# Attention blocks with (head, query) rows beside an LSTM recurrence, and an earlier output-gate product

## Chip, cores and metric

One core of a Trainium2 chip. The metric is the device time of one execution in microseconds, the median of three runs.

## The reference

Four sequences (B = 4) of S = 256 tokens with D = 128 features go through five stages; the last three are what the change is about.

1. An adaptive-layernorm transformer block in hyperbolic coordinates (16 heads), conditioned by one vector per sequence.
2. Causal attention with 16 heads of 8 features:

```python
Q, K, V = (x @ W_dq) @ W_uq, (x @ W_dkv) @ W_uk, (x @ W_dkv) @ W_uv      # each (B, S, 16, 8)
scores = einsum('bqhd,bkhd->bhqk', Q, K) / sqrt(8)
out = einsum('bhqk,bkhd->bqhd', softmax(where(causal, scores, -inf)), V).reshape(B, S, 128) @ W_o
```

3. The sum x + out, input of an LSTM of 128 units over the 256 tokens: `a = x_t @ Wx + b + h @ Wh`, then sigmoid and tanh gates. Step t needs h of step t - 1, and x_t needs the attention's output of token t.
4. A feed-forward block (128 to 512 to 128, GELU) on the LSTM's outputs, and a residual sum.

All tensors are float32.

## The kernel before, in words

Each engine has its own instruction list; semaphores join them. `big` is one large SBUF buffer, `bank` all eight PSUM banks. TensorE executes a float32 product as two passes, which the profile lists as two weight loads and two matmuls; a "pass" below is one of them.

**The front** (up to about 187 us) is the first stage, tiles of 128 tokens: two times `front`, attention or feed-forward, `join` on VectorE and ScalarE, with TensorE between. While VectorE is in the second `front`, ScalarE prepares the attention's and the LSTM's weights (L656 to L677). At the end of the front, TensorE turns the output weights W_o (L1308), waits for ScalarE's copy of them (L692), multiplies them with Wx (`wox`, L1310), waits for `tanh_out`, and fills the gates of the first 32 steps: biases, x @ Wx, h0 @ Wh (L1343 to L1347). Then it turns the first stage's result (L1351, waits for the first half of `join`'s output, `cond_out` 1) and begins the attention.

**The recurrence** is the loop over t of 256 steps in each of four engines' lists. In a step TensorE adds h @ Wh to the gates (12 passes, L1562 to L1564), ScalarE takes three tanh (L774 to L778), VectorE the cell state (L1136), ScalarE its tanh (L781), VectorE the new h (L1144) and the history (L1146). After these instructions each engine's list has its **jobs** of step t (`pe_jobs`, `act_jobs`, `vec_jobs`), which run while the others are in the chain of the step.

**The attention** is one of these jobs. Queries go in blocks of 32 tokens, called chunk c = 0 to 7; chunk c must be ready, with the gates made from it, before step 32 c. A block has c + 1 key blocks of 32. Rows of a score tile are (sequence, query), 4 x 32 = 128. A unit is some heads of a block: 4 heads for c below 4, 2 heads from there on. Units start every three steps from step 3 (`unit_at`); 44 of them run beside the recurrence, the last one starts in step 132. A unit m has

- step 0: `m_scores`, mask product (L1431), then for each head and sequence a product 32 columns wide in its own quarter of the array (L1436, `tile_position`); weights are the queries in `qz`, zero outside the head's 8 feature rows, moving data the keys of the sequence;
- step 1: VectorE takes the row maxima (`m_max`, L1070); steps 2 and 3: ScalarE the exponentials (L720);
- step 5: `m_turn`, four transposes of 128 columns on TensorE (L1449), step 6: VectorE copies them from PSUM (`m_weights`, L1079, 512 columns);
- step 7: `m_values`, for each head and sequence a product of 9 columns, 8 features and the sum of the weights (L1468), 16 products in all; steps 8 and 10, in a block's last unit: `m_norm`, `m_turn_out`, `m_oT`.

As units begin every third step, scores and the copy fall on steps with t = 0 mod 3, maximum and values on 1 mod 3, transposes on 2 mod 3. Other TensorE jobs: ten projections of the second half of the tokens (`PROJ`, every third step from step 2); and for the next chunk's gates, in steps 10 to 15 and 26 to 30 of each chunk, three bias products (L1315 to L1319), four products with x (L1322) and four with the attention's output (L1325). From step 146 on the feed-forward block takes the attention's place. The first block (L1356 to L1408, units 0 and 1) stands before the loop, in a form of its own with (sequence, query) rows, values held as block-diagonal `vd`.

**Queues.** SP issues, in order, for each block c from 1 on 16 transfers from `qT` into the ring `qz` (L499), one per head, block c after the scores of block c - 2. They follow the q half's ScalarE copy (L709). GpSimd's list ends with the low part of Wh (L549).

## Time and profile before

| | us |
|---|---|
| median of 3 runs (626.53 to 628.70) | 627.6 |
| profiled execution, its own time | 629.12 |
| its span, first to last instruction | 627.2 |
| mean granted TensorE clock | 0.622 of 2.4 GHz |
| busy: PE / DVE / ACT | 475.4 / 367.3 / 302.9 |

How to read it: PE is TensorE's matmuls, PEld its weight loads, DVE VectorE, ACT ScalarE, POOL GpSimd, SPq the queue of SyncE. The clock in slices is in tenths of full speed; it has two levels, 2.4 GHz (9 or 10 tenths) and 1.2 GHz (5 tenths). Matmuls overlap in the pipeline, so busy times of PE are not sums of useful work. A group `x4` in a timeline is four neighbours merged.

### The profile page before, as it was taken

The page shows a single profiled execution, that of the slowest core. Times are in us where ns is not written, and L with a number is a line of the kernel's source. Part 1 is how long each engine was busy: PE and PEld are TensorE (multiplying, and loading weights), DVE is VectorE, ACT ScalarE, POOL GpSimd, SP SyncE. Part 2 cuts the span into 40 slices and gives each one's busy share as a digit, 9 for nine tenths or more (in the row PEclk, how much of TensorE's full clock was granted, in tenths as well). Part 3 has the DMA queues.
Part 4 walks back from the last instruction along what each step waited for, and adds up shares of the span by engine and source line. Part 5 has one row for each costly group of instructions (what it writes and reads, how often), then busy time and mean ns, then how long its engine had stood idle before and what let it go on. Part 6 is the DMA issues. An engine that isn't in the chain of part 4 may idle for free.

```text
span 627.2 us, 17942 instructions
## 1 busy us (share of the span) xinstructions
PE 475.4 (76%) x6687; PEld 324.1 (52%) x6687; DVE 367.3 (59%) x2035; ACT 302.9 (48%) x1356; POOL 15.8 (3%) x36
## 2 busy tenths in 40 slices
PE   5973999107647898899999999898677768757746
PEld 2233334104535677666767666565455556545534
DVE  5367333894674556766676666666645555555553
ACT  4165785432324555645454444444454444444443
POOL 5000100030000000000000000000000000000000
PEclk9995999656957558855655555665555555555555
DMA  7200200000000000000000000000000000000000
GB/s 190 68 0 9 60 1 1 1 0 1 1 1 4 9 8 5 6 7 3 5 5 3 6 3 2 3 3 2 3 2 5 6 6 1 7 6 3 4 6 5
DMA packets 10884, 7.20 MB, mean 11 GB/s; under 512 B 2629, under 2 KB 9773, under 8 KB 10798
## 3 DMA queue, kind: packets, MB, share of 16 engines
q1 hardware_dynamic: 9742, 5.54, 3.5%
q8 instruction: 53, 0.87, 0.6%
q10 hardware_dynamic: 1056, 0.52, 0.3%
q14 instruction: 33, 0.27, 0.1%
HBM read 4.02 MB, written 0.52 MB: 7 GB/s over the span
## 4 chain that ended last, share of the span: by engine, by line
PE 54%; DVE 24%; ACT 15%; issue 5%; ACTq 0%; DVEq 0%
PE bank L1436 10%; PE bank L1562 7%; ACT hid_a L781 5%; DVE cell L1136 5%; PE bank L1449 5%; DVE hid L1144 4%; ACT keep L774 4%; PE bank L1322 3%; PE bank L1218 3%; PE bank L1564 3%; DVE cell_a L1128 2%; PE bank L1325 2%; PE bank L1206 2%; PE bank L1563 2%; PE bank L1162 2%
## 5 line engine op out<-in xcount | busy, mean ns | idle before, releaser
L1562 PE MATMUL bank<-hid,wha 128*128 128x4 f16 x1020 | 109.5, 173 | 70.1 <-DVE hid L1144 66.0
L1562 PEld LDWEIGHTS bank<-hid,wha 128*128 128x128 f16 x1020 | 89.1, 104 | 126.8 <-DVE hid L1144 120.3
L774 ACT ACTIVATE keep<-bank 128x4 f32<-128x4 f32 x256 | 44.4, 173 | 141.7 <-PE bank L1564 138.8
L1128 DVE SCALAR_TENSOR_TENSOR cell_a<-keep,cell 128x4 f32<-128x4 f32 x256 | 42.8, 167 | 110.9 <-ACT keep L774 109.6
L1563 PE MATMUL bank<-hid,whb 128*128 128x4 f16 x1020 | 103.6, 167 | 0.0
L1564 PE MATMUL bank<-hid,whn 128*128 128x4 f16 x1020 | 103.5, 166 | 0.0
L1563 PEld LDWEIGHTS bank<-hid,whb 128*128 128x128 f16 x1020 | 91.3, 107 | 2.2 <-issue 0.6
L781 ACT ACTIVATE hid_a<-cell 128x8 f32<-128x8 f32 x256 | 54.3, 212 | 73.8 <-DVE cell L1136 73.8
L1564 PEld LDWEIGHTS bank<-hid,whn 128*128 128x128 f16 x1020 | 87.3, 103 | 0.0
L1144 DVE TENSOR_TENSOR_SCAN hid<-hid_f,hid_a 128x20 f16<-128x20 f32 x256 | 51.2, 200 | 52.6 <-ACT hid_a L781 52.4
L1436 PE MATMUL bank<-kT,big 128*32 128x64 f32 (+6 forms) x896 | 66.4, 454 | 0.0
L1136 DVE TENSOR_TENSOR_SCAN cell<-cell_f,cell_a 128x16 f32<-128x16 f32 x256 | 49.1, 192 | 6.2 <-ACT cell_f L778 1.8
L778 ACT ACTIVATE cell_f<-bank 128x8 f32<-128x8 f32 x256 | 47.0, 184 | 0.3 <-PE bank L1325 0.3
L1449 PE MATMUL bank<-ident,p_mla 128*128 128x128 f32 (+3 forms) x176 | 44.5, 403 | 1.7 <-DVE qT L1090 1.7
L776 ACT ACTIVATE emit<-bank 128x4 f32<-128x4 f32 x256 | 44.3, 173 | 0.0
L1131 DVE TENSOR_SCALAR hid_f<-emit 128x8 f32<-128x8 f32 x256 | 43.7, 171 | 0.0
L1140 DVE RECIPROCAL hid_f<-hid_f 128x4 f32<-128x4 f32 x256 | 40.5, 158 | 0.4 <-issue 0.4
L720 ACT ACTIVATE p_mla<-bank,mx 128x64 f32<-128x64 f32 (+6 forms) x112 | 39.9, 378 | 0.0
L1436 PEld LDWEIGHTS bank<-kT,big 128*32 128x32 f32 x896 | 30.8, 156 | 12.9 <-issue 6.4
L1146 DVE TENSOR_TENSOR v_tm<-hid_f,hid_a 128x4 f32<-128x4 f32 x256 | 35.8, 140 | 0.1
L1468 PE MATMUL bank<-vaug,q_sq 128*32 128x9 f32 (+3 forms) x1408 | 31.3, 202 | 0.7 <-DVE q_sq L1079 0.5
L1079 DVE COPY q_sq<-bank 128x512 f32<-128x512 f32 (+3 forms) x46 | 30.9, 671 | 0.8 <-PE bank L1383 0.8
(271 smaller groups left out, 775.9 us busy)
## 6 DMA issues: line engine op xcount, KB each, us to landing
big<-qT SPq DMA_DIRECT2D x112, 4.0 KB
big<-big SPq DMA_DIRECT2D x16, 64.0 KB, 2.0
x_tm<-in_x ACTq DMA_DIRECT2D x2, 256.0 KB, 3.7
wf<-in_L_cond_w_f SPq DMA_DIRECT2D x2, 256.0 KB, 5.2
x_tb<-in_x SPq DMA_DIRECT2D x4, 128.0 KB, 2.8
out_y<-tb SPq DMA_DIRECT2D x7, 64.0 KB, 1.9
ada_w<-in_L_cond_w_ada SPq DMA_DIRECT2D x1, 384.0 KB
bf_all<-in_L_cond_b_f SPq DMA_DIRECT2D x1, 256.0 KB, 5.3
```

Source lines behind the costliest of these rows:

```text
L774: nc.scalar.activation(keep[:, k, :], keep_bank(c)[:, i], ACT.Tanh, scale=1.0 / A_SCALE).then_inc(keep_act, 1)
L776: nc.scalar.activation(emit[:, k, :], emit_bank(c)[:, i], ACT.Tanh, scale=1.0 / A_SCALE).then_inc(emit_act, 1)
L778: nc.scalar.activation(cell_f[:, k, :, 1:3].rearrange("p b s -> p s b"), new_bank(c)[:, i], ACT.Tanh, scale=1.0 / A_SCALE).then_inc(new_ac ...
L781: nc.scalar.activation(hid_a[:, k, :, 0:4:3], cell[:, k, :, 3].unsqueeze(2).to_broadcast([P, B, 2]), ACT.Tanh, scale=-1.0).then_inc(th_act, 1)
L1128: V.scalar_tensor_tensor(cell_a[:, k, :, 2], keep[:, k, :], 1.0, cell[:, 1 - k, :, 3], ALU.add, ALU.mult).then_inc(kept, 1)
L1136: V.tensor_tensor_scan(cell[:, k].rearrange("p b s -> p (b s)"), cell_f[:, k].rearrange("p b s -> p (b s)"), cell_a[:, k].rearrange("p b s ...
L1144: V.tensor_tensor_scan(hid[:, k].rearrange("p b s -> p (b s)"), hid_f[:, k].rearrange("p b s -> p (b s)"), hid_a[:, k].rearrange("p b s -> ...
L1436: ins = T.matmul(bank[q, m % 2, j * keys:(j + 1) * keys], qz[:, c % 2, heads[j], q], kT_tokens[:, b, 0:keys], start=False, stop=True, tile ...
L1449: ins = T.transpose(bank[0:rows, 2, i * P:(i + 1) * P], p_mla[:, m % 2, j * keys + kc * P:j * keys + kc * P + rows], ident[:])
L1562: T.matmul(acc, wha[:, gate, :], hid[:, k, :, 2], start=False, stop=True, skip_group_check=True)
L1563: T.matmul(acc, whb[:, gate, :], hid[:, k, :, 2], start=False, stop=True, skip_group_check=True)
L1564: ins = T.matmul(acc, whn[:, gate, :], hid[:, k, :, 4], start=False, stop=True, skip_group_check=True)
```

## The change

Score tiles of blocks 1 to 7 get rows (head r of a group, query), 4 x 32. A unit is now a group g of four heads (heads g, 4 + g, 8 + g, 12 + g) and all four sequences (blocks 1 to 3) or two of them (blocks 4 to 7). One product of full width, 128 columns, makes the scores of a sequence; half of them are issued in step 0, half in step 1. The exponentials are turned by VectorE in blocks of 32x32 from `p_mla` to `pt_mla` (step 5), which needs no TensorE transposes, no PSUM and no copy. The turned weights have keys of all four heads in the partitions, so the values are block-diagonal: `vd` holds for each sequence, key block and head its 32 x 9 values in that head's partitions and columns and zeros elsewhere; a value product has 36 columns, one for each key block and sequence, 32 wide, in step 8. `m_norm` moves to step 9, `m_turn_out` to 11, `m_oT` to 12.

`vd` is filled by SP: 12 transfers behind block 1's queries and 16 behind block 4's, 128 rows of 144 bytes each; the query transfers now move 32 pieces of 128 bytes instead of 8 of 512. GpSimd clears `vd` (8 memsets of 128x576 words, released by the first feed-forward product, and awaited by VectorE before the first block's values). The v projection of the first half moves from steps 2 and 5 to two places before the loop (`v_half`); the other projections move six steps up.

W_o is turned, copied and multiplied with Wx between the weight preparation's steps, during the second `front`; the first gates wait for `sq_in` (the scaled f2 output read out of its banks) instead of `tanh_out` and the late `wox`.

The diff, cut to its core:

```diff
-        UNITS = [(0, range(8 * i, 8 * i + 8)) for i in range(2)]
-        UNITS += [(c, range(h, h + n)) for c in range(1, CHUNKS) for n in [GROUP if c < GROUP else 2] for h in range(0, H, n)]
+        UNITS = [(0, 2 * i, None) for i in range(2)]
+        UNITS += [(c, g, range(b, b + n)) for c in range(1, CHUNKS) for n in [B if c < GROUP else B // 2] for g in range(NG) for b in range(0, B, n)]
-        PROJ = [("v", 0, 0), ("v", 0, 1), ("turn", 1, 0), ("turn", 1, 1), ("q", 1, 0), ("q", 1, 1), ("k", 1, 0), ("k", 1, 1),
+        PROJ = [("turn", 1, 0), ("turn", 1, 1), ("q", 1, 0), ("q", 1, 1), ("k", 1, 0), ("k", 1, 1),
@@ SP
-                    sp.dma_start(qz[rows, c % 2, h, :], flat(qT[rows])[:, c * P:(c + 1) * P]).then_inc(qz_fill[c % 2][h // GROUP], 16)
+                    r, g = divmod(h, GROUP)
+                    sp.dma_start(qz[rows, c % 2, :, g, QB * r:QB * r + QB], q_tokens[rows, c]).then_inc(qz_fill[c % 2][g], 16)
+                if c in (1, GROUP):
+                    f = c // GROUP
+                    if f == 0:
+                        sp.wait_ge(v_half_ready, 2)
+                        sp.wait_ge(vd_zero, 1)
+                        sp.wait_ge(ones_ready, 1)
+                    else:
+                        sp.wait_ge(proj_ready, len(PROJ))
+                    for kb in range(max(1, GROUP * f), GROUP * (f + 1)):
+                        for r in range(GROUP):
+                            keys = slice(QB * (kb % GROUP), QB * (kb % GROUP) + QB)
+                            sp.dma_start(vd[QB * r:QB * r + QB, :, kb, r].rearrange("p b g v -> p b (g v)"),
+                                         vm[keys, B * f:B * (f + 1), GROUP * r:GROUP * (r + 1), :].rearrange("p b h v -> p b (h v)")).then_inc(vd_fill[f], 16)
@@ GpSimd
+            pool.wait_ge(f1_mm, 1)
+            for b in range(B):
+                for c in range(0, CHUNKS, 4):
+                    ins = nc.gpsimd.memset(vd[:, b, c:c + 4], 0.0)
+            ins.then_inc(vd_zero, 1)
@@ ScalarE
             nc.scalar.activation(wdT[:], bank[0:64, 4, 0:P], ACT.Copy).then_inc(wdT_ready, 1)
+            act.wait_ge(wo_turned, 1)
+            nc.scalar.activation(woT, bank[:, 7, 0:P], ACT.Copy).then_inc(woT_ready, 1)
...
             nc.scalar.mul(h0[:], condT[:], H_SCALE).then_inc(w_ready, 1)
+            act.wait_ge(wox_mm, 1)
+            nc.scalar.activation(wox[:].rearrange("p g n -> p (g n)"), bank[:, 7, :], ACT.Copy).then_inc(wox_ready, 1)
...
-            act.wait_ge(wo_turned, 1)
-            nc.scalar.activation(woT, bank[:, 4, 0:P], ACT.Copy).then_inc(woT_ready, 1)
-            act.wait_ge(wox_mm, 1)
-            nc.scalar.activation(wox[:].rearrange("p g n -> p (g n)"), bank[:, 5, :], ACT.Copy).then_inc(wox_ready, 1)
...
+                if t in (0, 1):
+                    yield lambda: v_half(t)
@@ VectorE
-            go(V.tensor_copy(vd[:, :, :, HD], ...), vd_ready)
+            vec.wait_ge(vd_zero, 1)
+            for b in range(B):
+                go(V.tensor_copy(vd[:, b, 0, :, :, HD], ...), vd_ready)
...
             def m_weights(m):
-                V.tensor_copy(pt_mla[0:rows, m % 2, 0:cols], bank[0:rows, 2, ...][:, 0:cols]).then_inc(mt_ready, 1)
+                n = len(UNITS[m][2]) * keys_of(m)
+                vec.wait_ge(mp_ready, m + 1)
+                vec.wait_ge(mpv_mm, m - 1)
+                V.transpose(pt_mla[:, m % 2, 0:n], p_mla[:, m % 2, 0:n]).then_inc(mt_ready, 1)
@@ TensorE
             ins.then_inc(w_mla_mm, 1)
+            T.transpose(bank[:, 7, 0:P], wo_m[:], ident[:]).then_inc(wo_turned, 1)
             pe.wait_ge(ld_xtb, 64)
             turn8(lambda t: x_tb[:, t, :], 0, x_turned)
+            pe.wait_ge(woT_ready, 1)
+            pe.wait_ge(w_ready, 2)
+            T.matmul(bank[:, 7, :], woT, wx[:].rearrange("p g n -> p (g n)"), start=True, stop=True).then_inc(wox_mm, 1)
...
-            pe.wait_ge(tanh_out, 2)
-            pe.wait_ge(wox_ready, 1)
+            pe.wait_ge(sq_in, SQUARES_TO_F2)
...
+            def v_half(k):
+                for t in (2 * k, 2 * k + 1):
+                    ins = T.matmul(bank[:, 1, t * P:(t + 1) * P], vT[:, t, :], w_mla[:, 2, :], start=True, stop=True)
+                ins.then_inc(v_half_mm, 1)
             for m in range(FIRST_UNITS):
                 first_values(m)
+            v_half(0)
             m_turn_out(0)
+            v_half(1)
...
                 for j in range(n // 2 * part, n // 2 * (part + 1)):
-                    for b in range(B):
-                        q = slice(QB * b, QB * b + QB)
-                        ins = T.matmul(bank[q, m % 2, j * keys:(j + 1) * keys], qz[:, c % 2, heads[j], q], kT_tokens[:, b, 0:keys],
-                                       start=False, stop=True, tile_position=(0, QB * b), skip_group_check=True)
+                    ins = T.matmul(bank[:, m % 2, j * keys:(j + 1) * keys], qz[:, c % 2, bs[j], g, :], kT_tokens[:, bs[j], 0:keys],
+                                   start=False, stop=True, skip_group_check=True)
...
+                if m == FIRST_UNITS or (c == GROUP and g == 0):
+                    pe.wait_ge(vd_fill[c // GROUP], 16 * GROUP * (GROUP - 1 + c // GROUP))
+                for kb in range(c + 1):
+                    for j, b in enumerate(bs):
+                        at = (j * (c + 1) + kb) * QB
+                        n = GROUP * (HD + 1)
+                        ins = T.matmul(bank[QB * b:QB * b + QB, 4, n * g:n * (g + 1)], pt_mla[:, m % 2, at:at + QB], vd[:, b, kb, :, g, :],
+                                       start=(kb == 0), stop=(kb == c), tile_position=(0, QB * b))
...
+                for part, lag in ((0, 0), (1, 1)):
+                    m = unit_at(t, lag)
+                    if m is not None:
+                        yield lambda: m_scores(m, part)
+                n = unit_at(t, 8)
```

## Rows read from the trace of the kernel before

**Rows 1.** The page: busy time by engine, clock in 40 slices.
```profile
PE 475.4 (76%) x6687; PEld 324.1 (52%) x6687; DVE 367.3 (59%) x2035; ACT 302.9 (48%) x1356; POOL 15.8 (3%) x36
...
PEclk9995999656957558855655555665555555555555
```

**Rows 2.** Timeline, VectorE, L1144: start us, us, engine, line, operation, out<-in.
```profile
200.80 0.20 DVE L1144 TENSOR_TENSOR_SCAN hid<-hid_f,hid_a 128x20 f16<-128x20 f32 x1 [0.20 <-ACT hid_a L781]
...
476.49 0.20 DVE L1144 TENSOR_TENSOR_SCAN hid<-hid_f,hid_a 128x20 f16<-128x20 f32 x1 [0.20 <-ACT hid_a L781]
...
477.97 0.20 DVE L1144 TENSOR_TENSOR_SCAN hid<-hid_f,hid_a 128x20 f16<-128x20 f32 x1 [0.20 <-ACT hid_a L781]
...
620.03 0.20 DVE L1144 TENSOR_TENSOR_SCAN hid<-hid_f,hid_a 128x20 f16<-128x20 f32 x1 [0.20 <-ACT hid_a L781]
```

**Rows 3.** Timeline, TensorE, one attention unit of the last block.
```profile
431.25 1.09 PE L1449 MATMUL bank<-ident,p_mla 128*128 128x128 f32 x4
...
432.75 0.21 PE L1431 MATMUL bank<-mask,identb 128*128 128x64 bf16 x1
...
432.89 1.94 PE L1436 MATMUL bank<-kT,big 128*32 128x256 f32 x16
...
435.17 0.62 PE L1468 MATMUL bank<-vaug,q_sq 128*32 128x9 f32 x32
```

**Rows 4.** Timeline, VectorE, the same steps.
```profile
430.65 0.20 DVE L1144 TENSOR_TENSOR_SCAN hid<-hid_f,hid_a 128x20 f16<-128x20 f32 x1 [0.20 <-ACT hid_a L781]
...
430.82 0.69 DVE L1070 TENSOR_REDUCE mx<-bank 128x2 f32<-128x512 f32 x1
...
432.15 0.20 DVE L1144 TENSOR_TENSOR_SCAN hid<-hid_f,hid_a 128x20 f16<-128x20 f32 x1 [0.20 <-ACT hid_a L781]
...
433.63 0.20 DVE L1144 TENSOR_TENSOR_SCAN hid<-hid_f,hid_a 128x20 f16<-128x20 f32 x1 [0.20 <-ACT hid_a L781]
...
433.81 0.68 DVE L1079 COPY q_sq<-bank 128x512 f32<-128x512 f32 x1
...
435.98 0.20 DVE L1144 TENSOR_TENSOR_SCAN hid<-hid_f,hid_a 128x20 f16<-128x20 f32 x1 [0.20 <-ACT hid_a L781]
```

**Rows 5.** Timeline, TensorE, before the recurrence.
```profile
180.26 2.07 PE L1310 MATMUL bank<-wx,q_tm 128*128 128x512 f32 x2 [12.60 <-ACT q_tm L692]
...
183.36 0.80 PE L1322 MATMUL bank<-big,wx 128*128 128x128 f32 x2
...
187.41 1.09 PE L1351 MATMUL bank<-ident,v_tm 128*128 128x128 f32 x4
...
190.63 1.91 PE L1361 MATMUL bank<-w_mla,o_tm 128*128 128x128 f32 x8
```

**Rows 6.** Timeline, TensorE, the first block's values, and one pass of them.
```profile
196.57 0.34 PE L1393 MATMUL bank<-big,q_sq 128*32 128x36 f32 x16
...
L1393 PE MATMUL bank<-big,q_sq x32: 197/200/221, 196.6 to 197.3; 128*32 128x36 f32 x32
```

**Rows 7.** The page: the two scans; out<-in xcount | busy us, mean ns | idle before.
```profile
L1144 DVE TENSOR_TENSOR_SCAN hid<-hid_f,hid_a 128x20 f16<-128x20 f32 x256 | 51.2, 200 | 52.6 <-ACT hid_a L781 52.4
...
L1136 DVE TENSOR_TENSOR_SCAN cell<-cell_f,cell_a 128x16 f32<-128x16 f32 x256 | 49.1, 192 | 6.2 <-ACT cell_f L778 1.8
```

**Rows 8.** Timeline, VectorE, the last join, its first half of results.
```profile
182.69 1.14 DVE L943 SCALAR_TENSOR_TENSOR v_tm<-ta,small,tb 128x128 f32<-128x128 f32 x4
```

**Rows 9.** Windows: stretch, length, busy us of PE, PEld, DVE, ACT, POOL; PEclk, DMA share, GB/s.
```profile
183.80:193.40 9.60, 8.91 (x53) 7.72 (x52) 4.07 (x13) 3.42 (x11) 0.00 (x0) 0.50 0.00 0
193.40:200.20 6.80, 5.33 (x74) 3.06 (x66) 3.63 (x11) 2.23 (x7) 0.00 (x0) 1.00 0.02 5
```

**Rows 10.** SP's issues at L499 (ns min/median/max); landing of L484's transfers (us min/median/max).
```profile
L499 SPq DMA_DIRECT2D big<-qT x112: 624/624/1069, 196.3 to 356.1; - x112
...
DMA to landing us min/median/max: 2.0/2.0/2.2
```

**Rows 11.** Groups by line and shape: the weight loads of the eight products of rows 5.
```profile
L1361 PEld LDWEIGHTS bank<-w_mla,o_tm 128*128 128x128 f32 x8 | 1.8, 333 | 0.0
```

More of the change, by code:

```diff
@@ L224, in adaln_attention_lstm_ffn @@
         qz_zero = sem("qz_zero")
+        vd_zero = sem("vd_zero")
+        v_half_mm = sem("v_half_mm")
+        v_half_ready = sem("v_half_ready")
+        vd_fill = [sem("vd_fill_low"), sem("vd_fill_high")]
         ones_ready = sem("ones_ready")
@@ L365, in closes @@
         def closes(m):
-            return UNITS[m][1][-1] == H - 1
-        units_until = [sum(c <= k for c, _ in UNITS) for k in range(CHUNKS)]
+            return m == len(UNITS) - 1 or UNITS[m + 1][0] > UNITS[m][0]
+        units_until = [sum(c <= k for c, _, _ in UNITS) for k in range(CHUNKS)]
         ADA_PARTS = ((0, 2 * D), (2 * D, 6 * D))
@@ L418, in keys_of @@
             return QB * (UNITS[m][0] + 1)
-        def turns(m):
-            keys = keys_of(m)
-            return [(j, kc, min(P, keys - kc * P)) for j in range(len(UNITS[m][1])) for kc in range(1 + (keys > P))]
-        PROJ = [("v", 0, 0), ("v", 0, 1), ("turn", 1, 0), ("turn", 1, 1), ("q", 1, 0), ("q", 1, 1), ("k", 1, 0), ("k", 1, 1),
+        PROJ = [("turn", 1, 0), ("turn", 1, 1), ("q", 1, 0), ("q", 1, 1), ("k", 1, 0), ("k", 1, 1),
                 ("v", 1, 0), ("v", 1, 1)]
@@ L530, in _ @@
             pool.wait_ge(k_turned, NG)
-            for h in range(0, H, 4):
-                ins = nc.gpsimd.memset(qz[:, 1, h:h + 4], 0.0)
+            for b in range(B):
+                ins = nc.gpsimd.memset(qz[:, 1, b], 0.0)
             ins.then_inc(qz_zero, 1)
             pool.wait_ge(pv_mm, B * NG)
-            nc.gpsimd.memset(vaug[:, :, :, HD:HD + 1], 1.0).then_inc(ones_ready, 1)
+            nc.gpsimd.memset(vm[:, :, :, HD:HD + 1], 1.0).then_inc(ones_ready, 1)
             pool.wait_ge(w_ready, 4)
@@ L1066, in m_max @@
             def m_max(m):
-                keys, n = keys_of(m), len(UNITS[m][1])
+                keys, n = keys_of(m), len(UNITS[m][2])
                 vec.wait_ge(ms_mm, m + 1)
@@ L1420, in m_scores @@
             def m_scores(m, part):
-                c, heads = UNITS[m]
-                keys, n = keys_of(m), len(heads)
+                c, g, bs = UNITS[m]
+                keys, n = keys_of(m), len(bs)
                 if part == 0:
@@ L1438, in m_scores @@
                 if part == 1:
                     ins.then_inc(ms_mm, 1)
-            def m_turn(m, part):
-                keys = keys_of(m)
-                if part == 0:
-                    pe.wait_ge(mp_ready, m + 1)
-                    pe.wait_ge(mt_ready, m)
-                    pe.wait_ge(moT_ready, UNITS[m - 2][0] + closes(m - 2) if m > FIRST_UNITS + 1 else 1)
-                for i in (2 * part, 2 * part + 1):
-                    j, kc, rows = turns(m)[i]
-                    ins = T.transpose(bank[0:rows, 2, i * P:(i + 1) * P], p_mla[:, m % 2, j * keys + kc * P:j * keys + kc * P + rows], ident[:])
-                if part == 1:
-                    ins.then_inc(mt_mm, 1)
@@ L1453, in m_values @@
[L1453 to L1472 removed]
+            def m_values(m):
+                c, g, bs = UNITS[m]
+                pe.wait_ge(mt_ready, m + 1)
+                pe.wait_ge(mo_normed, c)
+                if m == FIRST_UNITS or (c == GROUP and g == 0):
[6 more added lines that the diff above has]
+                                       start=(kb == 0), stop=(kb == c), tile_position=(0, QB * b))
+                ins.then_inc(mpv_mm, 1)
```

124 lines of the change are left out of this document (51 added, 73 removed).

## The prediction

> **What bounds the kernel now.** I began with the page: TensorE is busy for 76% of the span, and its granted clock is at the lower level, 1.2 GHz, in most of the second half [rows 1]. That is an average over two parts, so the next view was VectorE's timeline at L1144, the last operation of each step of the recurrence. The first of the 256 stands at 200.80 us, the last at 620.03. Two neighbours with nothing beside them are 1.48 us apart [rows 2]. 255 such steps would take 377.4 us; they take 419.2. So 41.8 us lie in long steps, of which the stretch up to 477.97 (160 steps, 277.2 us against 236.8) has 40.4. This is where the attention runs beside the recurrence, and all that a better attention can win in the loop.
>
> Then one attention unit of the last block, step by step. TensorE's three jobs lie in three steps: mask and scores (432.75 to 434.83, 2.08 us), four transposes (1.09 us), values (0.62 us) [rows 3]. VectorE shows what each costs: the step with the transposes takes 1.50 us, 430.65 to 432.15, the next 1.48, and the one into which the scores reach 2.35, 433.63 to 435.98; the values lie in the step after, which is bare again [rows 4]. **Only the scores cost time**: 2.08 us of work lengthen a step by 0.87, so a step has room for 1.21 us of other TensorE work. VectorE's room ends similarly: its jobs begin 0.17 us after L1144 starts, and a 0.69 us maximum, over at 0.86, lengthens the step by 0.02. So a job may end 0.84 us after L1144 starts.
>
> **The change, part by part.** The 44 units, three steps apart, stay.
>
> *Transposes on TensorE, removed.* 4 per unit: worth nothing alone, since their step is bare. Cover: the room.
>
> *Scores.* Eight products 32 columns wide become two 128 wide, one in each of two steps. Four tiles shared the array before, so the work is about equal; the gain is the split. A 512-column float32 product takes 2.07 us in two passes and eight passes of 128 columns 1.91, or 0.24 each [rows 5], both at the lower clock; so a pass takes about its columns times two over 1.2 GHz, with its weight load hidden. The first part of a unit (mask 0.21, two passes, 0.2 for the first load and the tail) then takes 0.95, 1.05, 1.16 and 1.26 us for 160, 192, 224 and 256 keys; the second part 0.1 less. In blocks 1 to 3 there are four passes a part, of 0.21 to 0.24 us: 1.25 and 1.12. Against 1.21 this costs at most 0.05 a step.
>
> *Values.* 16 products of 9 columns become 2(c+1) of 36 in blocks 4 to 7, on only two of the four tiles at a time. The nearest row is the first block's: 16 passes of 36 columns on four tiles last 0.34 us at the upper clock, of which 0.20 is one pass [rows 6], so 0.01 each; at half the clock and half the tiles 0.03 to 0.04. For 20 to 32 passes I take 0.75, 0.87, 1.0 and 1.12 us: all inside the room. Bounds: 0.62, as now, and one tile at a time, 0.06 each, 1.9 us in block 7.
> The Trainium skill (TensorEngine Tiling (Array Packing), Instruction Overhead) says that a product of one free column lasts as long as one of 60; by it block 7's values would keep today's 0.62 us, an estimate that would take 1 us off the sum, in the steps that hold a gate product too.
>
> *Gate products beside the attention.* They stay, 8 per chunk, 0.80 us alone [rows 5], some 0.5 behind a full-width product that hides their load and 0.64 behind values; biases 0.3, the size of the mask's product. Now they are what does not fit: job plus 0.5 less 1.21. Block 4: 0.24, 0.14 and 0.13 in the three kinds of step; block 7: 0.55, 0.46 and 0.53. With the projections (now 8, in steps that also hold values) I sum 4.9 us in chunk 0, 1.7, 3.1 and 5.0 in chunks 1 to 3, and 2.0 in chunk 4.
>
> *VectorE.* The copy of 512 columns, 0.68 us [rows 4], becomes a block transpose of 256 to 512 columns from buffer to buffer, in a step of its own. No row shows one. Lower bound: the copy's rate, 1.3 ns a column. Upper bound: the costliest operation per column here, the scan, 20 against 16 columns in 200 against 192 ns, 2 ns a column [rows 7], so 1.18 us for 512. I take the copy's 0.68, the nearest in work: end at 0.85, nothing.
> The Trainium skill (VectorE: DVE Perf Modes, The three transpose paths) gives 311 ns for a 128x128 bf16 block transpose; if the 0.1 us over a plain operation of 128 columns is a fixed cost, an estimate, 512 columns take 0.78 and the sum grows by 1.3 us.
> The maximum now waits for the second part of the scores in the same step. In block 7 that ends 0.28 us into the window, so 0.32 + 0.69 = 1.01, 0.17 to 0.2 over: 1.6 us for the 8 units, and 0.6 for the 512-column maxima of block 3.
>
> *Loop:* 16.7 + 2.2 + 1.5 of the late steps, which stay, + 0.7 of ScalarE's gate blanks, which also stay, = 21.1 against 41.8: **20.7 us saved**.
>
> *Output-gate weights and first gates.* Now the wox product waits for ScalarE and takes 2.07 us from 180.26; the first gates follow from 183.4, and the transposes of the condition's result begin at 187.41, though VectorE has the first half at 183.83 [rows 5, 8]. With wox at about 126 us and the gates released at about 170, both in stretches where TensorE idles, the transposes start at 183.87: 3.5 us. Cover of the moved ScalarE copies: the statistics of the second front; without it 0.3 us.
> *What it gives back.* From 183.8 to 193.4 TensorE is busy for 8.9 of 9.6 us at 1.2 GHz; then to 200.2 it is granted 2.4 GHz [rows 9]. The work behind 190 moves ahead 3.5 us, the clock perhaps not: about 1.2 us. Two v halves (4 passes each) enter between values and first gates: 0.85 us each at the lower clock, behind VectorE's 0.5 and 0.3: 0.4. The fills of the block-diagonal values, two instructions, become eight smaller ones, some 0.3 us more, hidden behind the first scores. GpSimd's eight clears run where nobody waits for that queue. Net **1.5 us**, bounds 0.3 and 3.5.
>
> *SP's queue.* 12 copies for the values enter between block 1's queries and block 2's. An issue takes 0.62 us, at most 1.07 [rows 10], 0.67 apart. 28 from 196.31, where block 1's begin: the last is issued at 214.3 and lands 2.0 later, as today's copies within the buffers do, at 216.3. The first values of block 1 need it in step 11: 200.80, ten steps of 1.55 and 0.6, 216.9. Hidden by 0.6 us; block 2's queries by more. At 1.07 each the 12 come 4.8 later, 4.2 too late, and TensorE, waiting in order, holds the recurrence for it.
>
> **Sum.** 20.7 + 1.5 = 22.2 us. The profiled execution took 629.1 us (span 627.2, 1.9 around it), 1.5 over the median; it would be 606.9, and the median 627.6 - 22.2 = **605.4 us**. A difference of 0.3%, 1.9 us, is about what the measurement can tell.
>
> **Rivals.**
> 1. *The block transpose runs at the scan's rate.* Units then exceed the window by 0.13 (320 columns) to 0.51 (512), 13 us over 44 units, 1 of it beside TensorE's own excess: 617.5. For: nothing shows the operation. Against: every plain operation here takes 1.3 ns a column or less. 12%.
> 2. *Value products on two tiles don't overlap.* 0.06 us a pass: 0.2, 0.4, 0.7 and 0.9 over in blocks 4 to 7, times 8, and more with gate products: 18 us in all, less what fits beside: 619.5. For: all rows have four tiles in turn. Against: those overlap nearly fully, 16 passes of 256 columns in 1.94 us [rows 3] where one alone takes 0.43. 9%.
> 3. *Slower: the weight loads of the full-width scores are exposed.* 224 passes now load 128 float32 columns. If each load's 0.33 us [rows 11] stood before its pass, a part would take 1.8 us in blocks 1 to 3 and 1.7 in block 7: 15 us over in 12 units, 17 in 32, and gate products and projections in full, 20: a loop excess of 52 against 41.8, and 627.6 + 10.5 - 1.5 = 636.6. It decides at about 0.2 us exposed per pass. Against: the eight passes at 0.24 us each, loads of 0.33 in their records and all [rows 5, 11]. 6%.
> 4. *The values' copies come late:* 4.2 us, 609.6. 10%.
> 5. *The change saves only what the start gives,* because its smaller TensorE load costs the stretches of upper clock and the long steps stay: those are a few in the loop [rows 1], so at most some us: 626. 3%.
>
> **How the numbers follow.** My forecast has 60%; with its own errors (gate products between 0.3 and 0.64, start 0.3 to 3.5) it spans 598 to 613. To leave out no more than 2 in 10 the range takes in rivals 1, 2 and 4: 598 to 620. Faster: all but 3 and 5, and a part left for unseen waits: 0.90; same 0.03; slower 0.07.
>
> **What would show it.** Right: bare steps still 1.48 us; three steps of a block 7 unit within 0.3 us of 4.44 in sum, against 5.33 now; the first L1144 at about 199.3; the block transpose at 0.7 us for 512 columns; the two score parts of block 7 over 1.3 and 1.2 us; no gap of TensorE at the first values of block 1. Wrong: score products further apart than their columns, values at 1.9 us, a block transpose near 1.2, a stall on the values' copies at step 11, or long steps with VectorE's maximum as the last to end.

## The result and the profile after

The changed kernel takes 601.75 us, the median of 4 runs (601.33 to 602.05), against 627.07 for the kernel before, run beside it (625.97 to 628.7): a ratio of 0.9594, with a 95% interval of 0.957 to 0.9617. That is 25.3 us. Its profiled execution took 602.05 us with a span of 599.9, against 629.1 and 627.2 before.

The page answers to [rows 1]. TensorE has fewer and longer instructions and 23 us less of busy time. The upper clock (the level 2.4 GHz) is granted less often in the middle of the span, so the gain comes in spite of the clock there. The last line is the chain that ended last, by engine: SP's queue is in it with 3%, where it was not before.

```profile
PE 452.5 (75%) x5551; PEld 320.1 (53%) x5551; DVE 363.9 (61%) x2041; ACT 302.9 (50%) x1356; POOL 20.0 (3%) x44
...
PEclk9995999755977655555555555575555555555555
...
PE 48%; DVE 25%; ACT 16%; issue 5%; SPq 3%; DMA 1%; ACTq 0%; DVEq 0%
```

The timeline of VectorE at L1180, the same scan as L1144 in [rows 2] (start us, duration us, engine, line, operation):

```profile
196.08 0.20 DVE L1180 TENSOR_TENSOR_SCAN hid<-hid_f,hid_a 128x20 f16<-128x20 f32 x1 [0.20 <-ACT hid_a L811]
...
212.44 0.20 DVE L1180 TENSOR_TENSOR_SCAN hid<-hid_f,hid_a 128x20 f16<-128x20 f32 x1 [0.20 <-ACT hid_a L811]
...
216.78 0.20 DVE L1180 TENSOR_TENSOR_SCAN hid<-hid_f,hid_a 128x20 f16<-128x20 f32 x1 [0.20 <-ACT hid_a L811]
...
592.69 0.20 DVE L1180 TENSOR_TENSOR_SCAN hid<-hid_f,hid_a 128x20 f16<-128x20 f32 x1 [0.20 <-ACT hid_a L811]
```

A scan is the last operation of a step of the recurrence, so the distance of two scans is the length of a step. The first scan stands 4.7 us earlier than before, and the loop takes 396.6 us where it took 419.2: 22.6 saved. One step, from 212.44 to 216.78, takes 4.34 us. Added up over chunks of 32 steps the loop reads 54.6, 48.8, 50.0, 51.6, 49.5, 47.8, 48.1 and 46.3 us (31 steps in the last), where 32 bare steps are 47.4; before it was 55.5, 54.8, 56.6, 59.2, 51.2, 47.6, 48.4 and 46.1. The gain lies in chunks 1 to 3, 20 of the 22.6.

A unit of the last block, on TensorE (values, mask with the first score part, second part) and on VectorE, answers to [rows 3, 4]:

```profile
380.46 1.05 PE L1494 MATMUL bank<-big,q_sq 128*32 128x36 f32 x28
...
382.08 0.21 PE L1476 MATMUL bank<-mask,identb 128*128 128x64 bf16 x1
382.11 1.20 PE L1479 MATMUL bank<-kT,big 128*128 128x256 f32 x2
...
383.57 1.20 PE L1479 MATMUL bank<-kT,big 128*128 128x256 f32 x2
```

```profile
379.79 0.20 DVE L1180 TENSOR_TENSOR_SCAN hid<-hid_f,hid_a 128x20 f16<-128x20 f32 x1 [0.20 <-ACT hid_a L811]
...
380.15 0.69 DVE L1102 TENSOR_REDUCE mx<-bank 128x2 f32<-128x512 f32 x1
...
381.48 0.20 DVE L1180 TENSOR_TENSOR_SCAN hid<-hid_f,hid_a 128x20 f16<-128x20 f32 x1 [0.20 <-ACT hid_a L811]
...
381.65 0.70 DVE L1114 STREAM_TRANSPOSE q_sq<-p_mla 128x512 f32<-128x512 f32 x1
...
382.98 0.20 DVE L1180 TENSOR_TENSOR_SCAN hid<-hid_f,hid_a 128x20 f16<-128x20 f32 x1 [0.20 <-ACT hid_a L811]
...
384.45 0.20 DVE L1180 TENSOR_TENSOR_SCAN hid<-hid_f,hid_a 128x20 f16<-128x20 f32 x1 [0.20 <-ACT hid_a L811]
```

The three steps take 1.69, 1.50 and 1.47 us, 4.66 together, where they took 5.33. Neither score part lengthens the step that it reaches into (the second one reaches into the step of 1.69, but ends no later in its step than the first, whose step is bare). The 1.69 is VectorE's: the maximum starts 0.36 us after the scan, because the second part of the scores has only then ended, and is over at 1.05, 0.21 past the window. The block transpose takes 0.70 us and costs 0.02. Fewer than 32 value passes have a record here.

The long step of 4.34 us, on TensorE and in SP's own queue:

```profile
213.79 0.47 PE L1494 MATMUL bank<-big,q_sq 128*32 128x36 f32 x16 [2.09 <-DMA big<-vaug]
```

```profile
202.63 0.69 SPq L503 DMA_DIRECT2D big<-qT  x1
203.43 8.99 SPq L515 DMA_DIRECT2D big<-vaug  x12
```

TensorE stood still for 2.09 us until the last of the 12 copies for block 1's values had landed, and with it the recurrence, whose products stand in the same list.

The start, on TensorE, answers to [rows 5], and the windows (length, busy us of PE, PEld, DVE, ACT, POOL; PEclk, DMA share, GB/s) to [rows 9]:

```profile
125.71 2.04 PE L1314 MATMUL bank<-wx,q_tm 128*128 128x512 f32 x2 [1.90 <-ACT wx L694]
...
183.04 1.12 PE L1387 MATMUL bank<-ident,v_tm 128*128 128x128 f32 x4 [10.72 <-DVE v_tm L973]
```

```profile
183.00:188.10 5.10, 4.38 (x19) 3.80 (x19) 3.52 (x14) 2.66 (x9) 0.00 (x0) 0.50 0.00 0
188.10:198.40 10.30, 7.98 (x118) 5.27 (x116) 5.81 (x27) 4.78 (x20) 0.00 (x0) 1.00 0.03 5
```

VectorE's first half of the last join, which answers to L943 in [rows 8]:

```profile
181.85 1.14 DVE L973 SCALAR_TENSOR_TENSOR v_tm<-ta,small,tb 128x128 f32<-128x128 f32 x4
```

The transposes of the first stage's result start 4.4 us earlier, now as soon as VectorE has the first half: 1.19 us after L973 begins, where it was 4.72 after L943. So 3.5 us of the 4.4 come from the wait that is gone; in the other 0.8 VectorE itself was earlier (181.85 against 182.69). The upper clock comes at 188.1, 5.3 us earlier than before, and lasts 10.3 us instead of 6.8.

### The profile page after: what moved, and what is told of

Same layout as the page of the kernel before. It is cut to its first block, busy times and chain, and to the rows that moved or that the text cites. A ratio compares the mean times of both kernels' runs of the same rounds, so it can differ in the third digit from the quotient of the medians.

```text
span 599.9 us, 15671 instructions
## 1 busy us (share of the span) xinstructions
PE 452.5 (75%) x5551; PEld 320.1 (53%) x5551; DVE 363.9 (61%) x2041; ACT 302.9 (50%) x1356; POOL 20.0 (3%) x44
## 4 chain that ended last, share of the span: by engine, by line
PE 48%; DVE 25%; ACT 16%; issue 5%; SPq 3%; DMA 1%; ACTq 0%; DVEq 0%
PE bank L1479 8%; PE bank L1581 7%; ACT hid_a L811 5%; DVE cell L1172 5%; DVE hid L1180 4%; ACT keep L804 4%; PE bank L1254 3%; PE bank L1494 3%; PE bank L1359 3%; PE bank L1583 3%; PE bank L1242 2%; PE bank L1362 2%; PE bank L1582 2%; ACT cell_f L808 2%; PE bank L1198 2%
## 5 line engine op out<-in xcount | busy, mean ns | idle before, releaser
L1479 PE MATMUL bank<-kT,big 128*128 128x64 f32 (+6 forms) x224 | 92.1, 536 | 0.0
L1180 DVE TENSOR_TENSOR_SCAN hid<-hid_f,hid_a 128x20 f16<-128x20 f32 x256 | 50.9, 199 | 52.6 <-ACT hid_a L811 52.4
L1479 PEld LDWEIGHTS bank<-kT,big 128*128 128x128 f32 x224 | 53.8, 313 | 0.0
L808 ACT ACTIVATE cell_f<-bank 128x8 f32<-128x8 f32 x256 | 47.0, 184 | 0.3 <-PE bank L1362 0.3
L1494 PE MATMUL bank<-big,q_sq 128*32 128x36 f32 x1120 | 38.3, 254 | 2.1 <-DMA big<-vaug 2.1
L1494 PEld LDWEIGHTS bank<-big,q_sq 128*32 128x32 f32 x1120 | 31.9, 157 | 2.8 <-DVE q_sq L1114 2.2
L1102 DVE TENSOR_REDUCE mx<-bank 128x2 f32<-128x320 f32 (+6 forms) x44 | 25.5, 578 | 1.3
```

Of the source, the lines that this page charges most:

```text
L808: nc.scalar.activation(cell_f[:, k, :, 1:3].rearrange("p b s -> p s b"), new_bank(c)[:, i], ACT.Tanh, scale=1.0 / A_SCALE).then_inc(new_ac ...
L1180: V.tensor_tensor_scan(hid[:, k].rearrange("p b s -> p (b s)"), hid_f[:, k].rearrange("p b s -> p (b s)"), hid_a[:, k].rearrange("p b s -> ...
L1479: ins = T.matmul(bank[:, m % 2, j * keys:(j + 1) * keys], qz[:, c % 2, bs[j], g, :], kT_tokens[:, bs[j], 0:keys], start=False, stop=True, ...
L1494: ins = T.matmul(bank[QB * b:QB * b + QB, 4, n * g:n * (g + 1)], pt_mla[:, m % 2, at:at + QB], vd[:, b, kb, :, g, :], start=(kb == 0), sto ...
```

## The experiments

### The start and the loop apart

**The start alone, on the kernel before.** The output-gate product and the first gates are issued where the change has them; attention is as before.

```diff
             T.transpose(bank[:, 7, 0:P], wo_m[:], ident[:]).then_inc(wo_turned, 1)
+            pe.wait_ge(woT_ready, 1)
+            pe.wait_ge(w_ready, 2)
+            T.matmul(bank[:, 7, :], woT, wx[:].rearrange("p g n -> p (g n)"), start=True, stop=True).then_inc(wox_mm, 1)
...
-            pe.wait_ge(tanh_out, 2)
-            pe.wait_ge(wox_ready, 1)
+            pe.wait_ge(sq_in, SQUARES_TO_F2)
```

> The kernel before, with the earlier output-gate product and the earlier first gates alone. Theory: the start gives what it gave in the changed kernel, where the first L1144 stands 4.7 us earlier; the loop is that of before. Expected 622.3 us, 621.5 to 623.5, and the upper clock granted from about 188 us instead of 193. Rival: the 4.7 us came from elsewhere in the change (the v halves, other clock stretches by chance), and the start alone gives only the 3.6 us by which TensorE's transposes are released earlier, less 1.2 us of lost clock: 624.7 us or more.

Measured: 622.66 us (10 runs, 622.25 to 626.15) against 627.61, a ratio of 0.994 (0.9919 to 0.996): 5.0 us, with an interval from 2.5 to 5.1. The transposes and the clock of this kernel:

```profile
182.50 1.12 PE L1352 MATMUL bank<-ident,v_tm 128*128 128x128 f32 x4 [10.43 <-DVE v_tm L944]
```

```profile
187.20:194.00 6.80, 5.46 (x83) 3.16 (x82) 3.99 (x10) 2.94 (x9) 0.00 (x0) 1.00 0.02 4
```

The upper clock came 6.2 us earlier than in [rows 9] and lasted as long: it moved with the work, and nothing was given back: from the transposes to the first scan (195.71) it takes 13.2 us, where it took 13.4. The transposes come 3.5 us earlier relative to VectorE's join (L944 at 181.30), as in the change; the join itself was 1.4 us earlier in this execution.

**The change with its start undone** (the same edits backwards).

> The changed kernel with the output-gate product and the first gates back in their old places, the new attention kept. Theory: the parts add, so it loses what the start gave: 601.8 + 4.7 = 606.5 us, 605.5 to 607.5. Rival: part of the start's gain needs the late steps of the attention, or the step 11 wait for the values' copies shifts with it: under 605 us. That wait should be unchanged, about 2 us, since the copies and the loop start from the same moment.

Measured: 606.65 us (604.85 to 607.59), a ratio of 0.9665 (0.9642 to 0.9687). So the attention alone gives 21.0 us. The change did not run beside this kernel; its own ratios of 0.9594 and, later, 0.9615 put the start at 4.5 and 3.1 us.

The traces narrow the start down. From the beginning of the last join's first half to the first scan, the ten traces of this study with the earlier start take 14.1 to 14.6 us, the four with the old one 17.9 to 18.1. The start is worth 3.6 us by this. Where that join begins varies from 181.3 to 182.7 us in the ten and from 181.9 to 182.7 in the four, so what the medians show above 3.6 us is not shown to be the start's.

### What in the attention pays

**Both score parts in one step.**

```diff
-                for part, lag in ((0, 0), (1, 1)):
+                for part, lag in ((0, 0), (1, 0)):
```

> The changed kernel with both parts of a unit's scores in its first step. Theory: the split is the gain, full-width or not. In block 7 mask and four passes of 256 columns last 2.1 us, a step of 2.35 us as before; 0.2, 0.4, 0.65 and 0.87 us over in blocks 4 to 7, 17 us for 32 units; in blocks 1 to 3 eight passes of at least 0.21 us and the mask, 0.8 over, 10 us for 12 units; less 3 us of late maxima and about 3 us of gate products that now fit beside: 622 us, 619 to 626. Rival: the gain lies in the work itself being less (no transposes, no drains between tile shapes), and the step can take it: under 610 us.

Measured: 621.6 us (621.03 to 622.61), a ratio of 0.9908 (0.9886 to 0.993). A unit of block 7:

```profile
393.56 0.21 PE L1476 MATMUL bank<-mask,identb 128*128 128x64 bf16 x1
393.58 2.05 PE L1479 MATMUL bank<-kT,big 128*128 128x256 f32 x4
```

The four passes and the mask end 2.07 us after they began, as the old scores did in [rows 3], and the step from 394.44 takes 2.24 us. The start alone took 622.66 us beside it, so full-width products without the split are worth 1.1 us at most, and about 20 of the attention's 21 us are gone. It also measures the room of a step anew: 2.07 us of work cost 0.76, so this step had room for 1.31 us, not 1.21.

**The split alone, on the kernel before.** The old 32-column products, half of them a step later.

```diff
                     yield lambda: m_scores(m, 0)
-                    yield lambda: m_scores(m, 1)
+                if unit_at(t, 1) is not None:
+                    yield lambda: m_scores(unit_at(t, 1), 1)
```

> The kernel before with its scores split over two steps, everything else as it was. Theory: the split needs the steps that the transposes and the values held; the second half now stands beside the values (0.97 or 0.62 us) in one step. Block 7: 0.97 + 0.62 us of work and a room of 1.21, 0.4 over instead of 0.87; block 6 0.3 for 0.66; block 5 0.5 for 0.44; block 4 0.4 for 0.23: about 6 us less in all, 621 us, 618 to 624. Rival: the split alone is the gain, so most of the loop's 20 us show: 612 us or less.

Measured: 621.41 us (618.86 to 626.11), a ratio of 0.9907 (0.9879 to 0.9934), 6.2 us. The split alone gives less than a third of the attention's gain. What takes the rest is seen in a unit of its block 7: second score part and values in one train, the transposes alone in the next step (from 396.72 us on).

```profile
394.98 1.08 PE L1436 MATMUL bank<-kT,big 128*32 128x256 f32 x8
395.83 0.62 PE L1468 MATMUL bank<-vaug,q_sq 128*32 128x9 f32 x32
```

The step that holds both takes 1.81 us, two others 1.48 and 1.50. The old order had its bare step for the transposes; with the scores in two steps, the old kernel has four jobs for three steps. The change has three, because the transposes went to VectorE. So the parts need each other: the split pays in full only with the transposes gone.

**Three of four TensorE transposes left out, on the kernel before.** This kernel works on with stale turned weights.

```diff
-                for i in (2 * part, 2 * part + 1):
+                for i in ([] if part == 0 else [3]):
```

> The kernel before, which leaves out three of the four TensorE transposes of each unit beside the recurrence, so the values use stale turned weights. Theory: the transposes lie in steps with room for them; only gate products in the same steps gain, some 8 of them by up to 0.2 us, and the turn before an output copy: 625.5 us, 624.5 to 626.5. Rival: TensorE's work as such is the limit (it is busy for 76% of the span), 132 transposes of 0.27 us count in part, and over 10 us go.

Measured: 628.22 us (10 runs) against 628.01, a ratio of 0.9992 (0.9973 to 1.0011). Alone, the transposes' removal is worth nothing, where some 2 us were expected. In most steps that is because they had room: in block 7 their step is bare with them and without. In the loop's first steps it is a balance. Steps 6 to 20 and steps 21 to 35 of the kernel before, then of this one:

```profile
210.11:237.37 27.26, 25.17 (x516) 20.59 (x512) 16.36 (x102) 15.08 (x86) 0.00 (x0) 0.50 0.03 8
237.37:262.42 25.05, 21.25 (x555) 17.77 (x547) 17.59 (x104) 15.35 (x85) 0.00 (x0) 0.91 0.03 6
```

```profile
209.27:234.09 24.82, 21.68 (x501) 16.97 (x497) 16.37 (x102) 15.12 (x86) 0.00 (x0) 0.57 0.04 9
234.09:262.30 28.21, 25.03 (x536) 20.03 (x532) 17.91 (x104) 15.49 (x85) 0.00 (x0) 0.56 0.02 5
```

The first stretch is 2.4 us shorter, where transposes and gate products had shared steps. The second is 3.2 us longer, with a granted clock of 0.56 instead of 0.91. The stretch of upper clock that the kernel before has there is missing, in this kernel and in the profiled execution of the change; that the smaller load of TensorE is the reason is not shown.

### The stall on the copies

**A semaphore per key block.** Block 1's values then wait for the four copies of their own key block instead of all 12.

```diff
-                if m == FIRST_UNITS or (c == GROUP and g == 0):
-                    pe.wait_ge(vd_fill[c // GROUP], 16 * GROUP * (GROUP - 1 + c // GROUP))
+                if g == 0 and bs[0] == 0:
+                    pe.wait_ge(vd_fill[c], 16 * GROUP)
```

> The changed kernel with a semaphore for each key block's four value copies, so that block c's first value product waits for its own key block alone. Theory: the 2.1 us for which TensorE waits in step 11, behind all 12 copies, go, since the first four land some 6 us before they are needed: 599.5 us, 599.0 to 600.0. Rival: what waits is not the last copy but the queue in general, and block 2's queries, behind the 12 copies, are late next: 601 us or more, with a wait at step 15.

Measured: 601.39 us (600.82 to 602.31), 0.4 under the change where 2.2 were expected. The stall was gone from the trace (that step took 2.17 us), but steps 125 and 126 took 2.13 and 1.78 us, 0.7 more than in the change. The two kernels had not run beside each other, so both were run once more, side by side.

> The change once more, on the same chip and in the same rounds as the three kernels beside it, so that differences of 1 us can be read. Expected 601.8 us, as before; a ratio to the kernel before of 0.959.

> The change with a semaphore per key block for the values' copies, once more beside the change itself. My reading of the two traces: the stall of 2.2 us at step 11 goes, 0.6 us more comes from an upper clock at the end of the first chunk, and 0.8 us is lost at step 125, because the work there moves ahead of the stretch of upper clock. So 1.5 to 2 us under the change: 600.0. The rival, that the recurrence gives all of it back in slightly longer bare steps (1.483 against 1.479 us, 255 of them, 1 us), has less than 0.6 us between the two kernels.

Measured: the change 603.37 us (603.15 to 603.51), with the semaphores 599.87 (599.17 to 600.77), against 627.63. The steps around the stall, in this order:

```profile
213.66 0.20 DVE L1180 TENSOR_TENSOR_SCAN hid<-hid_f,hid_a 128x20 f16<-128x20 f32 x1 [0.20 <-ACT hid_a L811]
217.69 0.20 DVE L1180 TENSOR_TENSOR_SCAN hid<-hid_f,hid_a 128x20 f16<-128x20 f32 x1 [0.20 <-ACT hid_a L811]
```

```profile
212.29 0.20 DVE L1180 TENSOR_TENSOR_SCAN hid<-hid_f,hid_a 128x20 f16<-128x20 f32 x1 [0.20 <-ACT hid_a L811]
214.47 0.20 DVE L1180 TENSOR_TENSOR_SCAN hid<-hid_f,hid_a 128x20 f16<-128x20 f32 x1 [0.20 <-ACT hid_a L811]
```

The step falls from 4.03 to 2.18 us. The loop is 2.2 us shorter (394.3 against 396.5); the other 1.3 lie ahead of it (first scan at 195.9 against 197.3), where the two kernels are the same. The change itself came out 1.6 us apart in the two series, so a difference of 1 us between series says nothing. That and the two longer steps can have hidden the gain at first. Of the 3.5 us, 2.2 are what the semaphores are shown to give.

**The maximum, and all behind it, one step later** (with the semaphores; maximum, exponentials, transposes and norm at lags 2, 3, 4, 6, 10 and 13 instead of 1, 2, 3, 5, 9 and 12).

> As fill_by_block, and the maximum one step later, exponentials, block transpose, norm and the last copy with it, so that the maximum never waits for the second half of the scores in its own step. Theory: that wait costs 0.2 us in 12 steps of 512-column maxima and 0.04 in 8 of 448, and a transpose of 512 columns 0.02; some 2.8 us go: 596.7 us, 596.2 to 597.6. Rival: the maximum now ends last in another step (it meets no slack there), or the values move late: 599 us or more.

Measured: 602.74 us (600.54 to 602.88), a ratio of 0.9588 (0.9563 to 0.9612). That is 1.35 over the kernel with the semaphores alone, beside which it ran, with overlapping ranges; 2.8 under it were expected. The 0.21 us are gone from block 7's bare steps, but other steps are longer: in chunk 3 steps 119 and 122 take 1.99 and 2.13 us instead of 1.60 and 1.96, so the chunk stays at 52.4, and chunk 2 reads 50.4 us against 49.9. A job moved by a step frees one and fills another.

### The gate products

**The change without the gate products of chunks 1 to 7.**

```diff
-                elif i < 7:
-                    input_of(c, i - 3)
-                else:
-                    if i == 7:
-                        pe.wait_ge(moT_ready, c + 1)
-                    attended_of(c, i - 7)
+                elif i == 7:
+                    pe.wait_ge(moT_ready, c + 1)
```

> The change without the eight gate products of each chunk 1 to 7 (the x and the attended part; the bias products stay), so the gates lack these terms. It measures the term of my sum that was far too large. By the prediction's price (0.5 us behind a score part, 0.64 behind values, against a room of 1.21) about 14 us of the gate steps would go: 588. By the trace of the change the 34 long steps that hold a gate product in chunks 0 to 4 have 8.1 us over bare ones in all, of which projections, masks and maxima keep about 1: 594.5. If the gate products' load on TensorE also cost the clock, it would be less than either.

Measured: 598.84 us (598.56 to 599.74), a ratio of 0.9546 (0.9518 to 0.9574); its gates lack those terms. Both readings missed it. The trace shows 53 steps of 1.55 us, and they are just those whose products went. Two scans in a row, and the first weight load behind the first of them:

```profile
416.50 0.20 DVE L1180 TENSOR_TENSOR_SCAN hid<-hid_f,hid_a 128x20 f16<-128x20 f32 x1 [0.20 <-ACT hid_a L811]
418.05 0.20 DVE L1180 TENSOR_TENSOR_SCAN hid<-hid_f,hid_a 128x20 f16<-128x20 f32 x1 [0.20 <-ACT hid_a L811]
```

```profile
416.82 0.11 PEld L1577 LDWEIGHTS bank<-hid,wha 128*128 128x128 f16 x1 [1.15 <-ACT cell_f L808]
```

The load stands 0.32 us after the scan. What was left in these steps is the wait for the last tanh, now with no instruction of its own behind it, in front of the recurrence's wait.

**The same, with those waits left out too.**

```diff
-                if t % STEPS in INPUT_STEPS and t < S - STEPS:
+                if t % STEPS in INPUT_STEPS[:3] and t < S - STEPS:
```

> gates_left_out once more, and now the waits of those jobs (for the last tanh of the step, and for the attended rows) are left out with the products. The run before showed 53 steps of 1.55 us where bare ones take 1.48: TensorE's first weight load starts 0.31 us after the last scan instead of 0.25, only in the steps whose queue held the wait without its product. If a wait that stands alone in front of the recurrence's own wait costs 0.07 us, these steps are 1.48 again and 53 x 0.07 = 3.7 us go: a ratio of 0.9546 x 627.6 = 599.1 less 3.7, 595.4 us, and the price of the gate products by difference to the change (603.4 in the call before) is 8 us, what the long steps of the trace add up to. The rival, that TensorE's emptier steps themselves are slower to start (a lighter load, the lower clock throughout), leaves them at 1.55 and the time at 599.

Measured: 595.43 us (594.81 to 596.17), a ratio of 0.9489 (0.9467 to 0.9511).

```profile
416.46 0.20 DVE L1180 TENSOR_TENSOR_SCAN hid<-hid_f,hid_a 128x20 f16<-128x20 f32 x1 [0.20 <-ACT hid_a L811]
417.94 0.20 DVE L1180 TENSOR_TENSOR_SCAN hid<-hid_f,hid_a 128x20 f16<-128x20 f32 x1 [0.20 <-ACT hid_a L811]
```

```profile
416.71 0.10 PEld L1575 LDWEIGHTS bank<-hid,wha 128*128 128x128 f16 x1 [1.08 <-DVE hid L1180]
```

The load comes 0.25 us after the scan and the steps are 1.48 again: the lone wait cost 0.07 us a step. The rival of steps that are slower to start because they are emptier is excluded. The gate products of the loop, with their waits, cost 0.9615 less 0.9489 of 627.7, 7.9 us, give or take 2; the loops of the two traces differ by 7.4 (396.5 against 389.2).

**The first six gate jobs of a chunk kept out of the steps with mask and first score part** (with the semaphores).

```diff
-        INPUT_STEPS = [*range(10, 16), *range(26, 31)]
+        INPUT_STEPS = [[i for i in range(10, 19) if (STEPS * c + i) % 3 != 2][:6] + [*range(26, 31)] for c in range(CHUNKS)]
```

> fill_by_block with the first six of each chunk's gate jobs kept out of the steps in which the mask and the first score part stand (those steps are skipped, the six take the next free ones). In the trace of the change a gate product costs 0.41 to 0.53 us beside the mask and first part in blocks 5 and 6, and 0.12 to 0.33 beside the second part. Five such steps (14, 47, 77, 110, 140) change: 0.15 + 0.3 + 0.3 + 0.2 + 0.3 us, some 1.2 us under the kernel with the semaphores alone: 598.8 if that one is at 600.0. Rival: the jobs behind them (values beside a gate product, 0.2) take it back: no difference.

Measured: 597.9 us (597.64 to 599.6) against 599.87 without this edit beside it, a ratio of 0.9534 (0.9504 to 0.9563). The loop is 1.4 us shorter (392.9 against 394.3), near the 1.2 expected. It is the fastest version of this study that leaves nothing out, 29.7 us under the kernel before.

## Why the prediction was right, and where it was not

The sign and the mechanism held, and 601.75 lies in the range, 3.7 us under the number given. By its own steps:

**What bounds the kernel: right.** Bare steps are still 1.48 us. A part of 1.23 us with its mask costs nothing in block 7. The room of 1.21 us was read from the old scores; behind full-width products it is 1.31, as shown below.

**Scores: right.** Forecast 1.16 to 1.26 us a part with the mask; 1.20 to 1.23 measured. The rival of exposed weight loads is excluded: the loads have mean records of 0.31 us and a 256-column pass 0.65, and two passes end 1.20 us after the first began. **Transposes off TensorE worth nothing alone: right as a total,** shown by the kernel that left them out, though in the first chunk by a balance with the clock; and the step did not say that they are what makes room for the split, which the other kernels show.

**Values: near.** 1.12 us forecast for block 7; 1.05 in the row above, and up to 1.18 elsewhere in the block. It stays inside the room, and the rival of two tiles that don't overlap (1.9 us) is excluded. What doubled the time is the number of tiles, not the columns. Block 3 has 32 passes of 36 columns on four tiles, block 7 has 32 on two, both at the lower clock:

```profile
254.32 0.71 PE L1494 MATMUL bank<-big,q_sq 128*32 128x36 f32 x32
...
385.12 1.18 PE L1494 MATMUL bank<-big,q_sq 128*32 128x36 f32 x32
```

On four tiles 9 columns took 0.62 us [rows 3] and 36 take 0.71; on two tiles 36 take 1.18. The Trainium skill (TensorEngine Tiling (Array Packing), Instruction Overhead) says that a product of one free column lasts as long as one of 60. This trace comes near to it with the tiles unchanged (0.09 us in 32 passes); the prediction's sentence, by which block 7 would stay at 0.62, left the halved number of tiles out.

**Block transpose: right.** The groups by shape (busy us, mean ns):

```profile
L1114 DVE STREAM_TRANSPOSE q_sq<-p_mla 128x512 f32<-128x512 f32 x12 | 8.4, 703 | 0.0
...
L1114 DVE STREAM_TRANSPOSE q_sq<-p_mla 128x256 f32<-128x256 f32 x4 | 1.7, 436 | 0.0
```

0.68 us was taken for 512 columns; it is 0.70, 1.04 ns a column and 0.17 fixed. The copy was the right row to go by; the estimate of 0.78 from the page on DVE Perf Modes in the Trainium skill was too high. **Late maximum: right,** 0.21 us against 0.17 to 0.2.

**Gate products: mis-sized, 16.7 us forecast against some 12.5.** The excess of chunks 0 to 4 over bare steps is 17.7 us; 2.2 of it are the stall, some 2.0 the maxima, 1.0 one late step. The step of the prediction that failed is "job plus 0.5 less 1.21", in both numbers. Two score parts of block 6, each with a gate product behind it:

```profile
343.54 1.09 PE L1479 MATMUL bank<-kT,big 128*128 128x224 f32 x2
344.42 0.63 PE L1362 MATMUL bank<-qT,wox 128*128 128x128 f32 x2
344.85 0.21 PE L1581 MATMUL bank<-hid,wha 128*128 128x4 f16 x1
...
345.21 1.09 PE L1479 MATMUL bank<-kT,big 128*128 128x224 f32 x2
346.10 0.63 PE L1362 MATMUL bank<-qT,wox 128*128 128x128 f32 x2
```

```profile
344.39 0.20 DVE L1180 TENSOR_TENSOR_SCAN hid<-hid_f,hid_a 128x20 f16<-128x20 f32 x1 [0.20 <-ACT hid_a L811]
346.09 0.20 DVE L1180 TENSOR_TENSOR_SCAN hid<-hid_f,hid_a 128x20 f16<-128x20 f32 x1 [0.20 <-ACT hid_a L811]
347.78 0.20 DVE L1180 TENSOR_TENSOR_SCAN hid<-hid_f,hid_a 128x20 f16<-128x20 f32 x1 [0.20 <-ACT hid_a L811]
```

The first gate product ends at 345.05, 0.42 us behind the end of the score part (344.63), and the second 0.43; 0.5 was forecast. The first train begins with the mask at 343.51 and lasts 1.54 us; the step that it reaches into takes 1.70, 0.22 over, so the room is 1.32. The second lasts 1.52 for 0.21 over: 1.31 again, as in the kernel with both score parts in one step. The forecast's room of 1.21 comes from a job of 32-column products. The recurrence's first pass begins 0.20 us before such a full-width train ends (344.85 against 345.05), and began 0.07 before the old scores ended (434.76 against 434.83). For these two steps the forecast's way gives 0.45 and 0.35 us over; they have 0.22 and 0.21. The whole of the loop's gate products was then measured at 7.4 to 7.9 us; chunk 0's projections and small excesses of single steps are the rest of the term.

**Start: mis-sized. 1.5 us forecast, 3.6 by the traces of all kernels, 5.0 in the runs with an interval from 2.5 to 5.1.** The 3.5 us that the transposes gain are exactly as forecast. The step that failed is "the work behind 190 moves ahead 3.5 us, the clock perhaps not: about 1.2 us". The upper clock moved ahead with the work in the change and in the start alone. From the transposes to the first scan it takes 13.0 us in the change, where it took 13.4, so the v halves, for which 0.4 was charged, cost nothing that shows either. The prediction's own terms, 3.5 less 1.2 less 0.4, add up to 1.9, not to its 1.5. In the two profiled executions the first scan moved by 4.7 us; 0.8 of that is the earlier join of VectorE, which differs as much between executions of kernels with the same start.

**SP's queue: wrong in sign, 2.1 us.** "Hidden by 0.6 us" became a wait of 2.09. The issues' beginning relative to the first scan was as forecast, 4.49 us before it. But the 16 queries take 11.84 us (191.59 to 203.43) and the 12 copies 8.99, 0.74 and 0.75 apart instead of 0.67, which is 2.1 late; and the steps before the need take 1.48 us, not 1.55, so that it comes 0.5 earlier. The issues by line (ns min/median/max, first and last start in us):

```profile
L503 SPq DMA_DIRECT2D big<-qT x112: 685/686/1175, 191.6 to 342.7; - x112
```

```profile
L515 SPq DMA_DIRECT2D big<-vaug x28: 595/602/1512, 203.4 to 262.2; - x28
```

One of the twelve took 1.43 us, and each query now 0.69 instead of 0.62. The rival of the late copies, given 10%, so came true by half beside the forecast: 2.1 of its 4.2 us.

**Sum.** The two profiled executions are 27.3 us apart in span where 22.2 were forecast, 5.1 more. The stretch before the first scan gave 3.2 of it (0.8 by the earlier join), the loop 1.9: 4.2 of the gate products, less the stall's 2.2, with smaller terms that nearly cancel. The medians moved by 25.3 only, since the profiled execution of before lay 2 us over its median in that series, not 1.5, and the profiled one of the change 0.3 over. So the forecast's closeness owes something to luck: it put the gain of two terms too low, by 4.2 and by some 2.1 us, and a wait that it had ruled out took 2.2 back. Two slips of its working change no reading: 0.75 us of values in block 4 with 0.64 behind them are 0.18 over the room, not 0.13, and rival 2's excesses are some 0.2 us a unit larger than its own 0.06 us a pass gives.

## What to carry to other kernels

Beside a recurrence that bounds the time, count the jobs per step, not the busy time: a job costs only what exceeds the room of its step, so splitting one pays if a step is free for its second half, and taking one away from a step that had room for it pays nothing unless another moves into its place. Measure that room with the kind of job that is to fill it: it was 1.21 us behind the old products and 1.31 behind the new. A margin of 0.6 us over 28 issues of one queue is no margin: price the slowest member of the group, and let a wait name only the transfers that it needs. A difference of 1 us between two variants is read only when both run side by side.

## What was not expected of the hardware

A wait that stands by itself in TensorE's queue, in front of the next wait, costs 0.07 us on the path even though the tanh that it waits for was over before the scan that the step waits for began: 53 steps of 1.55 us with it, 1.48 without. The profile names the stale releaser (the tanh at L808) where the true one is the scan. Work that moved ahead took its stretch of upper clock with it, in both kernels with the earlier start. What stays open is why the start of identical kernels differs by up to 1.4 us between executions; the stretch of upper clock in the second front began at 152.3 us in one and at 150.2 in the other, which goes with it and is not shown to be its cause.
